# A residual conv block on one core: one pair recomputed in the last pass instead of two, a second pair of sums spilled and reloaded

## The chip, the cores and the metric

The kernel runs on one core of one Trainium2 chip. The metric is the device time of one execution in microseconds. The median of 3 runs of the kernel before is 548.7 us, the lowest 547.78 and the highest 549.61.

## The reference

The input x is float32 of shape (32, 64, 56, 56). The block computes x + relu(BN2(conv2(relu(BN1(conv1(g))))) + g), where g is x after a group norm of 32 groups (two channels in a group):

```python
identity = x
out = conv3x3(x, quantize_weight(w1, W_BITS), b1)
out = jax.nn.relu(batchnorm(out, gamma1, beta1))
out = conv3x3(out, quantize_weight(w2, W_BITS), b2)
out = batchnorm(out, gamma2, beta2)
out = jax.nn.relu(out + identity)
...
x = x + _L0_conv_ref(_gn(x), ...)
```

Both batch norms take their mean and variance over all 32 images, so that nothing of the output can be made before the second convolution of every image is done.

## The kernel before

**Pairs.** Two images of 64 channels fill the 128 partitions. There are NP = 16 such pairs; the data of one are 128 x 3136 float32, 1568 KB. Each conv splits its float32 input into a high and a low float16 part and runs 9 taps x 4 quadrants x 2 parts = 72 matmuls in each of 4 rounds (7 rows of each half image) that make a pair's sums in PSUM.

**Three passes.** Pass one loads x, takes the group norm statistics (DVE), splits (ACT makes the high part, DVE the low one), convolves, and keeps conv1's output in one of RES = 13 slots of SBUF; 3 pairs go out to DRAM (`y1_spill`). Pass two does the same with conv2 in the order `PAIR2`; its sums are put in the slots. Its last 3 steps need the pairs that were spilled, and they are loaded over the sums of steps 0, 1 and 2. Pass three, from the end of conv2 on, loads x again for each pair, computes relu(scale * sums + skip * x + bias) + x, and stores it. `ORDER3` gives the conv2 step that each turn u of pass three takes; "pair u" below is the pair of turn u. `x3[u]` is where its x is loaded.

**Where the 16 sets of sums are in pass three.** Pair 1's (`IN_PSUM`) stay in PSUM. Of the three sets that were overwritten, step 2's was stored to DRAM (`y2_spill`, L387) and is loaded back for pair 15 (`RELOADED`, L464). Steps 0 and 1 were lost: these are pairs 7 and 10 (`AGAIN`), and both convolutions are computed again for them from x. The other 12 sets are in slots.

**Three ways through pass three.**

- Ring pairs (1, 2, 3, 4, 11 to 15): ACT seeds a PSUM bank with scaled x (`seed`, L759), PE adds the sums through a diagonal matrix (`add_sums`, L1406), DVE finishes (`finish`, L1224). This is done in 4 rounds a pair, a bank each.
- Two-pass pairs (0, 5, 6, 8, 9), which need no PSUM: ACT scales the sums in place (`two_affine`, L747), DVE adds x (`sum_and_add`, L1202) and does the relu and the second addition (`relu_and_add`, L1208). Pair 0 is done in 5 pieces, the others in two halves. Pair 5's x lies partly in the spare ends of the slots (`IN_STRIPS`) and is loaded there early, during conv2.
- Recomputed pairs (7, 10): ACT makes act in float32 (`make_act1`, L775) and its high half (`make_hi1`, L781), DVE the low half (`again_low1`, L1230), PE convolves in 4 rounds (`again_round1`, L1429 and L1433), ACT and DVE split each round (`make_act2`, L792 and L794; `again_low2`, L1235), PE convolves again (`again_round2`, L1452) and adds x through `add_parts` (L1414), ACT seeds (`seed_again`, L799), DVE finishes (L1224).

**Transfers.** All loads and stores of pass three are issued by SP, in one order that is written out by hand (L443 to L478). SP waits ahead of each one for what it needs: a store for DVE's result, a load for the buffer to be free, either because DVE has read it (`wait_out`) or because a store out of it has landed (`wait_stored`). What stands behind a waiting transfer in this order waits with it. The orders of ACT (L802 to L846), DVE (L1239 to L1267) and PE (L1477 to L1496) are written out in the same way.

```python
            def wait_stored(u):
                sp.wait_ge(stored[u], 16 * STORES[u])

            def wait_out(u):
                if u in TWO_PASS:
                    sp.wait_ge(two_out, first_two(u) + 2)
                else:
                    sp.wait_ge(ring_out, nth(u, NQ - 1))
```

Of the kernel before, what the change touches and what calls it, by code (L numbers as in the profile page):

```python
# [23 lines left out]
def conv_block_kernel(nc, x, w1, b1, g1, be1, w2, b2, g2, be2, out):  # L24
# [61 lines left out]
    with ExitStack() as ctx:  # L86
# [262 lines left out]
        def _(sp):  # L349
# [70 lines left out]
            def store_first():  # L420
                for k in range(PARTS0):
# [5 lines left out]
            def store_two_pass(u):
                for k in range(2):
                    cols = half_of(u, k)
                    sp.wait_ge(two_out, first_two(u) + k + 1)  # L430
                    sp.dma_start(pair_view(out, PAIR3[u])[:, cols], out_of(u)[:, cols]).then_inc(stored[u], 16)
# [1089 lines left out]
```

## Time and profile before

| what | value |
|---|---|
| median of 3 runs | 548.7 us |
| the profiled execution's own time | 549.96 us |
| its span in the trace | 548.2 us |
| PE busy | 505.5 us (92%) |
| DVE busy | 442.6 us (81%) |
| ACT busy | 367.9 us (67%) |
| DMA of SP's queue (q1) | 91.19 MB, 44.7% of 16 engines' span |
| mean granted TensorE clock | 0.977 |

The span is cut into 40 equal slices on the page, of 13.7 us each. The end of conv2 lies in the 30th of them; the last ten hold pass three. Busy shares over the whole span mix passes with different limits, so pass three has to be read by itself, in stretches.

### The profile page before, as it was taken

Reading aid. Unit: us, or ns where it says so; the run is one execution under the profiler, and the core shown is the slowest. Engines: PE = TensorE matmul, PEld = TensorE weight load, DVE = VectorE, ACT = ScalarE, POOL = GpSimd, SP = SyncE. Lnnn points to the kernel's source line nnn. Section 1 sums busy time; section 2 is a strip of 40 time slices with the busy share of each in tenths; the row PEclk is TensorE's granted clock in tenths of the full one; section 3 lists DMA queues with packets and bytes.
Section 4 is the critical chain, followed back from the end, with each engine's and each line's share of the span. In section 5 each row is a group of like instructions: output and inputs, shape, how many; then the busy total and the mean of one; then the engine's idle time right before and its main releaser. Section 6 shows DMA issues by size and latency. Waiting matters only on the chain.

```text
span 548.2 us, 23785 instructions
## 1 busy us (share of the span) xinstructions
PE 505.5 (92%) x11037; PEld 429.0 (78%) x11037; DVE 442.6 (81%) x628; ACT 367.9 (67%) x402; POOL 96.4 (18%) x155
## 2 busy tenths in 40 slices
PE   3999999999999999999999999999968598999970
PEld 1899899999998896998988888888854277685540
DVE  8899989999999658988868988787869376896760
ACT  3799899989999845755665555566227577774650
POOL 2026366665662200210000000000010000000000
PEclk9899999999999999999999999999999899999995
DMA  8834775333441000002344000000659969299997
GB/s 289 322 126 128 271 274 178 133 125 131 162 160 58 8 7 7 4 2 121 130 158 181 26 4 2 4 4 4 205 221 354 381 245 325 98 359 426 416 423 314
DMA packets 24474, 92.99 MB, mean 170 GB/s; under 512 B 8248, under 2 KB 9656, under 8 KB 20664
## 3 DMA queue, kind: packets, MB, share of 16 engines
q1 hardware_dynamic: 24192, 91.19, 44.7%
q8 instruction: 86, 1.41, 1.1%
q10 hardware_dynamic: 184, 0.30, 0.2%
q14 instruction: 12, 0.10, 0.1%
HBM read 58.27 MB, written 32.28 MB: 165 GB/s over the span
## 4 chain that ended last, share of the span: by engine, by line
PE 84%; DMA 6%; DVE 4%; issue 2%; ACT 1%; SPq 0%; DVEq 0%; ACTq 0%
PE conv_ps L1310 69%; DMA slots<-in_x_dram 5%; PE conv_ps L1452 5%; PE conv_ps L1429 4%; PE conv_ps L1406 3%; DVE slots L1208 1%; PE conv_ps L1414 1%; DMA out_dram<-slots 1%; DVE slots L1202 1%; PE conv_ps L1273 1%; ACT split L591 0%; DVE small L920 0%; ACT conv_ps L759 0%; DVE slots L1224 0%; PE conv_ps L1308 0%
## 5 line engine op out<-in xcount | busy, mean ns | idle before, releaser
L1310 PE MATMUL conv_ps<-split,wmat 64*64 64x385 f16 (+3 forms) x9216 | 381.8, 325 | 1.6 <-ACT split L591 1.6
L1310 PEld LDWEIGHTS conv_ps<-split,wmat 64*64 64x64 bf16 x9216 | 342.8, 108 | 36.7 <-issue 2.3
L625 ACT ACTIVATE slots<-conv_ps,par,evac_scale 128x784 f32<-128x784 f32 x124 | 123.8, 999 | 96.2 <-PE conv_ps L1310 94.2
L1021 DVE BATCH_NORM_STATS2 bn_tup<-slots 128x6 f32<-128x392 f32 x166 | 81.9, 556 | 15.6 <-ACT slots L625 15.6
L920 DVE BATCH_NORM_STATS2 small<-slots 128x6 f32<-128x448 f32 x112 | 61.8, 615 | 0.7 <-DMA slots<-in_x_dram 0.7
L988 DVE TENSOR_TENSOR split<-slots,split 128x3136 f16<-128x3136 f32 (+4 forms) x36 | 57.2, 1608 | 4.6 <-ACT slots L599 1.0
L990 DVE SCALAR_TENSOR_TENSOR split<-slots,split 128x3248 f16<-128x3248 f32 (+3 forms) x18 | 53.6, 2979 | 2.3
L1406 PE MATMUL conv_ps<-slots,bn_tup 128*128 128x392 f32 x128 | 45.5, 516 | 9.9 <-ACT conv_ps L759 9.8
L1406 PEld LDWEIGHTS conv_ps<-slots,bn_tup 128*128 128x128 f32 x128 | 25.2, 199 | 30.0 <-issue 14.0
L974 DVE TENSOR_SCALAR slots<-slots,bn_w 128x3248 f32<-128x3248 f32 (+3 forms) x18 | 30.4, 1687 | 20.9 <-ACT split L583 20.5
L583 ACT ACTIVATE split<-slots,bn_w 128x3248 f16<-128x3248 f32 x14 | 43.1, 3082 | 0.0
L633 ACT ACTIVATE xa<-conv_ps,par,evac_scale 128x784 bf16<-128x784 f32 x40 | 39.7, 995 | 0.0
L1224 DVE SCALAR_TENSOR_TENSOR slots<-conv_ps,slots 128x784 f32<-128x784 f32 x20 | 19.4, 973 | 25.1 <-PE conv_ps L1406 14.4
L583 ACT ACTIVATE split<-slots,gn_b_all,gn_s_all 128x3136 f16<-128x3136 f32 x12 | 35.9, 2994 | 0.0
L546 POOL MEMSET bn_tup<- 128x192 f32 x1 | 0.3, 257 | 169.5 <-DVE bn_mv L1036 169.5
L974 DVE TENSOR_SCALAR slots<-slots,gn_s_all,gn_b_all 128x3136 f32<-128x3136 f32 (+4 forms) x19 | 26.4, 1396 | 1.5 <-ACT split L583 1.3
L526 POOL TENSOR_SCALAR small<-small 128x1 f32<-128x1 f32 x14 | 24.2, 1726 | 1.2
L591 ACT ACTIVATE split<-slots,gn_b_all,gn_s_all 128x784 f16<-128x784 f32 (+3 forms) x20 | 17.5, 901 | 0.6 <-DVE gn_b_all L951 0.6
L1308 PE MATMUL conv_ps<-split,wmat 64*64 64x55 f16 (+1 forms) x192 | 17.8, 187 | 0.0
L799 ACT ACTIVATE conv_ps<-conv_ps,again_w,bn_w 128x784 f32<-128x784 f32 x8 | 7.8, 975 | 14.6 <-PE conv_ps L1452 14.6
L515 POOL TENSOR_TENSOR small<-small 128x1 f32<-128x1 f32 x14 | 3.9, 278 | 77.4 <-DVE small L932 77.4
L524 POOL TENSOR_SCALAR small<-small 128x1 f32<-128x1 f32 x14 | 17.1, 1222 | 1.5
(161 smaller groups left out, 468.5 us busy)
## 6 DMA issues: line engine op xcount, KB each, us to landing
slots<-in_x_dram SPq DMA_DIRECT2D x51, 392.0 KB, 5.1
slots<-in_x_dram SPq DMA_DIRECT2D x10, 1568.0 KB, 9.3
out_dram<-slots SPq DMA_DIRECT2D x16, 784.0 KB, 14.5
split<-in_x_dram SPq DMA_DIRECT2D x4, 1568.0 KB, 15.3
out_dram<-slots SPq DMA_DIRECT2D x4, 1568.0 KB, 18.9
y_spill<-slots SPq DMA_DIRECT2D x3, 1624.0 KB, 7.0
slots<-y_spill SPq DMA_DIRECT2D x3, 1624.0 KB, 6.8
xa<-in_x_dram SPq DMA_DIRECT2D x3, 1568.0 KB, 9.7
```

What stands on the lines that cost most here:

```text
L526: nc.gpsimd.tensor_scalar(tmp(5), tmp(4), -0.5 * GN_GAIN, 1.5 * GN_GAIN, ALU.mult, ALU.add).then_inc(gn_pool, 1)
L583: nc.scalar.activation(whole(hi_of(t), ph), whole(slot_of(ph, t), ph), func, bias=bias, scale=scale).then_inc(hi_ready[ph], NQ)
L625: nc.scalar.activation(dst, src, ACT.Identity, bias=bias, scale=scale, accum_out=total).then_inc(evacuated[ph], 1)
L633: nc.scalar.activation(squares[n % 2], conv_ps[:, BUF[q], :, 0:CH], ACT.Square, bias=par[:, 0:1], scale=evac_scale[:, 0:1], accum_out=ysum ...
L920: ins = nc.vector.bn_stats(gn_tup[:, m, n, :], slots[:, t % RES, n * GN_CHUNK:(n + 1) * GN_CHUNK])
L974: ins = nc.vector.tensor_scalar(a, s, scale, bias, ALU.mult, ALU.add)
L988: ins = nc.vector.tensor_tensor(l, a, h, ALU.subtract)
L990: ins = nc.vector.scalar_tensor_tensor(out=l, in0=a, scalar=0.0, in1=h, op0=ALU.max, op1=ALU.subtract)
L1021: ins = nc.vector.bn_stats(bn_tup[:, 2 * (n - first) + s, :], rows[s])
L1310: return nc.tensor.matmul(bank[:, r0:r1, w0:w1], lhs, rows[:, top + r0:top + r1, w0 + kx - 1:w1 + kx - 1], start=n == 0 and part is hi_all ...
L1406: mm = nc.tensor.matmul(sums_in(k)[:, h], scale_diag, ys[:, h], start=False, stop=True, skip_group_check=True)
L1452: return nc.tensor.matmul(bank[:, r0:r1, w0:w1], lhs, rows[:, top + r0:top + r1, w0 + kx - 1:w1 + kx - 1], start=n == 0 and part == 0, sto ...
```

## The change

Pair 10 is no longer recomputed. A second set of conv2's sums is stored to DRAM during conv2, and two sets are loaded back in pass three, for the last two pairs (14 and 15). `AGAIN` holds pair 7 alone. Its x is loaded into `xa` during conv2, where pair 3's was; pair 3's x comes in five pieces behind the stores of pair 0, where pair 4's did. The two-pass pairs are 0, 4, 5 and 6: pair 4 was a ring pair, 8 and 9 become ring pairs. Pairs 4, 5 and 6 are done in halves between the rounds of pair 7. The order of the ring and of SP's transfers, and the buffers `x3`, are written anew to fit.

```diff
-    AGAIN = (7, 10)
-    RELOADED = NP - 1
-    ORDER3 = (SPILL, NP - 1, *range(SPILL + 1, SPILL + 6), 0, SPILL + 6, SPILL + 7, 1, *range(SPILL + 8, NP - 1), 2)
+    AGAIN = (7,)
+    RELOADED = {NP - 2: 4, NP - 1: 5}
+    ORDER3 = (SPILL, NP - 1, *range(SPILL + 1, SPILL + 6), 0, *range(SPILL + 6, NP - 1), 1, 2)
...
-    SLOT3 = [None if u == IN_PSUM or u in AGAIN else SLOT2[ORDER3[5 if u == RELOADED else u]] for u in range(NP)]
+    SLOT3 = [None if u == IN_PSUM or u in AGAIN else SLOT2[ORDER3[RELOADED.get(u, u)]] for u in range(NP)]
...
-    TWO_PASS = (0, 5, 6, 8, 9)
+    TWO_PASS = (0, 4, 5, 6)
...
-    STORES = [PARTS0, 2, 2, 2, 1, 2, 2, 2, 2, 2, 2, 1, 1, 1, 2, 4]
+    STORES = [PARTS0, 2, 2, 2, 2, 2, 2, 2, 1, 1, 1, 1, 1, 1, 2, 4]
...
-    IN_STRIPS = 5
+    IN_STRIPS = 4
...
-            slots[:, FREE], halves[0], halves[1], xa, slots[:, FREE], xa, slot3(2), slot3(0), xa, slot3(2), slots[:, FREE],
-            halves[0], halves[1], xa, slot3(2), slot3(0))]
-        again1 = [ap.bitcast(F16)[:, 0:2 * PIX].rearrange("p (h m) -> p h m", h=2) for ap in (halves[0], slot3(3))]
...
+            slots[:, FREE], halves[0], halves[1], slots[:, FREE], slot3(0), slots[:, FREE], slot3(2), xa, slot3(3), slot3(0),
+            slots[:, FREE], slot3(2), halves[0], halves[1], xa, slot3(3))]
...
-            for t in range(SPILL):
-                sp.wait_ge(evacuated[1], NQ * (t + 1))
-            sp.dma_start(y2_spill, slots[:, SLOT2[SPILL - 1], 0:PIX]).then_inc(y2_spilled, 16)
+            for n in range(SPILL - 1):
+                sp.wait_ge(evacuated[1], NQ * (n + 2))
+                sp.dma_start(y2_spill[n], slots[:, SLOT2[n + 1], 0:PIX]).then_inc(y2_spilled[n], 16)
             for t in range(SPILL):
                 sp.wait_ge(evacuated[1], NQ * (t + SPILL + 1))
                 sp.wait_ge(bn_seen[1], NQ * (t + 1))
-                if t == SPILL - 1:
-                    sp.wait_ge(y2_spilled, 16)
+                if t >= 1:
+                    sp.wait_ge(y2_spilled[t - 1], 16)
                 sp.dma_start(slots[:, SLOT2[NP - SPILL + t]], y1_spill[t]).then_inc(y1_loaded[t], 16)
...
-            load(3)
+            load(7)
...
-                    sp.dma_start(x3[4][:, cols], pair_view(x, PAIR3[4])[:, cols]).then_inc(x3_loaded[4], 16)
...
+                    sp.dma_start(x3[3][:, cols], pair_view(x, PAIR3[3])[:, cols]).then_inc(x3_loaded[3], 16)
+
+            def store_half(u, k):
+                cols = half_of(u, k)
+                sp.wait_ge(two_out, first_two(u) + k + 1)
+                sp.dma_start(pair_view(out, PAIR3[u])[:, cols], out_of(u)[:, cols]).then_inc(stored[u], 16)
...
+            def reload_sums(n):
+                u = NP - 2 + n
+                wait_stored(RELOADED[u])
+                sp.wait_ge(y2_spilled[n], 16)
+                sp.dma_start(slot3(u)[:, 0:PIX], y2_spill[n]).then_inc(y2_loaded[n], 16)
...
             store_first()
             store_ring(1)
             wait_stored(0)
-            load(7)
+            load(4)
             store_ring(2)
             store_ring(3)
             wait_out(3)
             load(5)
             wait_stored(2)
             load(6)
-            store_ring(4)
+            store_half(4, 0)
+            wait_stored(3)
+            load(8)
+            store_half(4, 1)
             wait_out(4)
+            load(9)
+            store_half(5, 0)
+            store_half(5, 1)
+            wait_out(5)
             load(10)
-            store_two_pass(5)
-            wait_out(5)
-            load(8)
-            store_two_pass(6)
+            reload_sums(0)
+            store_half(6, 0)
+            store_half(6, 1)
             wait_out(6)
-            load(9)
-            wait_stored(5)
-            sp.wait_ge(y2_spilled, 16)
-            sp.dma_start(slot3(RELOADED)[:, 0:PIX], y2_spill).then_inc(y2_loaded, 16)
+            load(11)
+            reload_sums(1)
             store_ring(7)
             wait_out(7)
-            load(11)
             load(12)
-            store_two_pass(8)
+            load(13)
+            store_ring(8)
             wait_out(8)
-            load(13)
-            store_two_pass(9)
-            wait_out(9)
+            load(15)
+            wait_stored(7)
             load(14)
-            wait_stored(7)
-            load(15)
-            for u in range(10, NP):
+            for u in range(9, NP):
                 store_ring(u)
...
             make_act1(0)
-            seed(4, 0)
-            seed(4, 1)
             make_hi1(0)
-            seed(4, 2)
-            seed(4, 3)
+            two_affine(4, 0)
+            two_affine(4, 1)
+            make_act2(0, 0)
             two_affine(5, 0)
+            make_act2(0, 1)
             two_affine(5, 1)
-            make_act2(0, 0)
+            make_act2(0, 2)
             two_affine(6, 0)
-            make_act2(0, 1)
+            make_act2(0, 3)
             two_affine(6, 1)
-            make_act2(0, 2)
-            make_act2(0, 3)
-            seed_again(0, 0)
-            make_act1(1)
-            seed_again(0, 1)
-            make_hi1(1)
-            seed_again(0, 2)
-            two_affine(8, 0)
-            seed_again(0, 3)
-            two_affine(8, 1)
-            make_act2(1, 0)
-            two_affine(9, 0)
-            make_act2(1, 1)
-            two_affine(9, 1)
-            make_act2(1, 2)
-            make_act2(1, 3)
             for q in range(NQ):
-                seed_again(1, q)
-            for u in range(11, NP):
+                seed_again(0, q)
...
-            dve.wait_ge(x3_loaded[4], 16 * PARTS0)
-            finish(4, 0)
-            finish(4, 1)
             again_low1(0)
-            finish(4, 2)
-            finish(4, 3)
-            for r in range(2):
-                u = (5, 8)[r]
-                for q in range(NQ):
-                    two_pass(u, q)
-                    again_low2(r, q)
-                for q in range(NQ):
-                    two_pass(u + 1, q)
-                    finish(AGAIN[r], q)
-                    if (r, q) == (0, 1):
-                        again_low1(1)
-            for u in range(11, NP):
+            two_pass(4, 0)
+            two_pass(4, 1)
+            again_low2(0, 0)
+            two_pass(4, 2)
+            again_low2(0, 1)
+            two_pass(4, 3)
+            two_pass(5, 0)
+            again_low2(0, 2)
+            two_pass(5, 1)
+            again_low2(0, 3)
+            two_pass(5, 2)
+            two_pass(5, 3)
+            finish(7, 0)
+            two_pass(6, 0)
+            finish(7, 1)
+            two_pass(6, 1)
+            two_pass(6, 2)
+            finish(7, 2)
+            two_pass(6, 3)
+            finish(7, 3)
+            for u in range(8, NP):
...
-                pe.wait_ge(ring_out, nth((4, AGAIN[0])[r], q))
+                pe.wait_ge(ring_out, nth(3, q))
...
-            for u in (2, 3, 4):
+            for u in (2, 3):
...
-            again_round1(1, 0)
             add_parts(0, 3)
-            for q in range(1, NQ):
-                again_round1(1, q)
-            again_round2(1, 0)
-            for q in range(1, NQ):
-                again_round2(1, q)
-                add_parts(1, q - 1)
-            add_parts(1, 3)
-            for u in range(11, NP):
+            for u in range(8, NP):
```

Along with these, `y2_spill`, `y2_spilled` and `y2_loaded` are made twofold, and the waits for pair 7's inputs name the new neighbours.

How the instructions stand on the engines, in pass three. First SP's transfers. Before, from the stores of pair 1 to those of pair 9 (L441 and L431 are stores, L397 loads of x, L464 the reload):

```order
L441 DMA out_dram<-slots 128x1568 x4
L397 DMA xa<-in_x_dram 128x1680
L397 DMA slots<-in_x_dram 128x3136
L441 DMA out_dram<-slots 128x3136
L397 DMA slots<-in_x_dram 128x3136
L431 DMA out_dram<-slots 128x1456
L431 DMA out_dram<-slots 128x1680
L397 DMA xa<-in_x_dram 128x3136
L431 DMA out_dram<-slots 128x1568 x2
L397 DMA slots<-in_x_dram 128x3136
L464 DMA slots<-y_spill 128x3136
```

And in the changed kernel, from the stores of pairs 2 and 3 to the second reload (L446 and L430 are the stores, L436 the reloads):

```order
L446 DMA out_dram<-slots 128x1568 x4
L397 DMA slots<-in_x_dram 128x3136 x2
L430 DMA out_dram<-slots 128x1456
L397 DMA slots<-in_x_dram 128x3136
L430 DMA out_dram<-slots 128x1680
L397 DMA slots<-in_x_dram 128x3136
L430 DMA out_dram<-slots 128x1568 x2
L397 DMA slots<-in_x_dram 128x3136
L436 DMA slots<-y_spill 128x3136
L430 DMA out_dram<-slots 128x1568 x2
L397 DMA slots<-in_x_dram 128x3136
L436 DMA slots<-y_spill 128x3136
```

Behind the two loads that follow pair 3's stores, SP now waits for half a two-pass pair (128x1456), not for a whole ring pair; and ahead of pair 6's two stores (the last x2 of halves in each fence) it issues five loads of x and a reload, where it issued four loads, one of them of 128x1680.

Second, DVE's order from the end of pair 3 or 4 on. Before (L1224 finishes a round, L1230 and L1235 belong to the recomputed pair, L1202 and L1208 to two-pass pairs):

```order
L1224 SCALAR_TENSOR_TENSOR slots<-conv_ps,slots 128x784 x2
L1230 TENSOR_TENSOR split<-split 128x3136
L1224 SCALAR_TENSOR_TENSOR slots<-conv_ps,slots 128x784 x2
L1202 SCALAR_TENSOR_TENSOR slots<-slots,skip_s 128x1456
L1235 SCALAR_TENSOR_TENSOR split<-conv_ps,split 128x2x448
L1208 SCALAR_TENSOR_TENSOR slots<-slots 128x1456
L1235 SCALAR_TENSOR_TENSOR split<-conv_ps,split 128x2x392
L1202 SCALAR_TENSOR_TENSOR slots<-xa,skip_s,slots 128x1680
L1235 SCALAR_TENSOR_TENSOR split<-conv_ps,split 128x2x392
L1208 SCALAR_TENSOR_TENSOR slots<-slots,xa 128x1680
```

In the changed kernel the same place reads (L1208 finishes a round, L1214 and L1219 belong to the recomputed pair, L1186 and L1192 to two-pass pairs):

```order
L1208 SCALAR_TENSOR_TENSOR slots<-conv_ps,slots 128x784 x4
L1214 TENSOR_TENSOR split<-split 128x3136
L1186 SCALAR_TENSOR_TENSOR slots<-slots,skip_s 128x1456
L1192 SCALAR_TENSOR_TENSOR slots<-slots 128x1456
L1219 SCALAR_TENSOR_TENSOR split<-conv_ps,split 128x2x448
L1186 SCALAR_TENSOR_TENSOR slots<-slots,skip_s 128x1680
L1219 SCALAR_TENSOR_TENSOR split<-conv_ps,split 128x2x392
L1192 SCALAR_TENSOR_TENSOR slots<-slots 128x1680
L1186 SCALAR_TENSOR_TENSOR slots<-slots,skip_s 128x1568
L1219 SCALAR_TENSOR_TENSOR split<-conv_ps,split 128x2x392
```

No ring round stands between the low half and the rounds of the recomputed pair any more, and the first two-pass half is finished ahead of the first split of a round instead of around it.

## Rows read from the trace of the kernel before

**Rows 1.** The page's second part: the span in 40 slices, DMA's busy tenths and GB/s.

```profile
DMA  8834775333441000002344000000659969299997
GB/s 289 322 126 128 271 274 178 133 125 131 162 160 58 8 7 7 4 2 121 130 158 181 26 4 2 4 4 4 205 221 354 381 245 325 98 359 426 416 423 314
```

**Rows 2.** Busy time in stretches of pass three; the header names the columns.

```profile
core 0: us, PE busy (x) PEld busy (x) DVE busy (x) ACT busy (x) POOL busy (x), PEclk, DMA share, GB/s
409.50:415.00 5.50, 5.19 (x11) 2.86 (x12) 5.40 (x8) 5.50 (x7) 0.27 (x1) 0.69 0.71 221
415.00:440.00 25.00, 16.65 (x45) 9.00 (x44) 13.71 (x15) 15.88 (x14) 0.00 (x0) 0.88 1.02 390
440.00:450.00 10.00, 10.00 (x215) 7.60 (x217) 7.88 (x6) 6.93 (x7) 0.00 (x0) 0.95 0.47 196
450.00:465.00 15.00, 13.44 (x312) 12.17 (x303) 10.96 (x8) 12.05 (x11) 0.00 (x0) 1.00 0.95 321
465.00:480.00 15.00, 14.13 (x350) 10.00 (x352) 12.33 (x9) 11.37 (x9) 0.00 (x0) 1.00 0.30 121
480.00:505.00 25.00, 24.23 (x505) 17.76 (x498) 19.39 (x15) 14.15 (x15) 0.00 (x0) 1.00 1.01 390
505.00:546.50 41.50, 26.48 (x80) 14.74 (x78) 21.20 (x22) 17.99 (x19) 0.00 (x0) 0.88 0.97 402
```

**Rows 3.** What SP's queue waited for, 440 to 480 us: total, times, longest.

```profile
SPq L431 <- DVE slots L1208: 29.0, 4, 10.7
```

**Rows 4.** SP's issues in order of time: start, length, line, transfer, count.

```profile
249.41 0.33 SPq L387 DMA_DIRECT2D y_spill<-slots  x1
...
452.81 7.20 SPq L431 DMA_DIRECT2D out_dram<-slots  x2
460.06 0.46 SPq L397 DMA_DIRECT2D xa<-in_x_dram  x1
467.96 11.39 SPq L431 DMA_DIRECT2D out_dram<-slots  x2
479.39 0.46 SPq L397 DMA_DIRECT2D slots<-in_x_dram  x1
```

**Rows 5.** ACT in order of time around 425 to 440 us.

```profile
425.30 1.01 ACT L759 ACTIVATE conv_ps<-xa,skip_b,skip_s 128x784 f32<-128x784 f32 x1 [0.31 <-DVE slots L1224]
432.09 3.00 ACT L775 ACTIVATE split<-slots,again_w,gn_s_all 128x3136 f32<-128x3136 f32 x1 [5.78 <-DMA slots<-in_x_dram]
...
436.87 2.98 ACT L781 ACTIVATE split<-slots,again_w,gn_s_all 128x3136 f16<-128x3136 f32 x1
```

**Rows 6.** The chain that ended last, 475 us to the end: start, length, what.

```profile
478.69 9.09 PE conv_ps L1429 x214
487.78 6.12 PE conv_ps L1452 x141
...
506.41 14.58 DMA slots<-in_x_dram
522.17 10.79 PE conv_ps L1406 x32
```

**Rows 7.** DVE's operations of the stretch, one of each kind, in order of time.

```profile
442.36 3.42 DVE L1230 TENSOR_TENSOR split<-split 128x3136 f16<-128x3136 f32 x1
...
453.48 0.97 DVE L1235 SCALAR_TENSOR_TENSOR split<-conv_ps,split 128x784 f16<-128x784 f32 x1 [0.69 <-ACT conv_ps L794]
...
460.44 1.84 DVE L1202 SCALAR_TENSOR_TENSOR slots<-slots,skip_s 128x1568 f32<-128x1568 f32 x1
465.26 0.97 DVE L1224 SCALAR_TENSOR_TENSOR slots<-conv_ps,slots 128x784 f32<-128x784 f32 x1 [2.98 <-PE conv_ps L1414]
466.15 1.78 DVE L1208 SCALAR_TENSOR_TENSOR slots<-slots 128x1568 f32<-128x1568 f32 x1
```

**Rows 8.** Busy time in three stretches of 5 us, for PEclk.

```profile
430.00:435.00 5.00, 0.00 (x0) 0.00 (x0) 0.53 (x1) 2.91 (x1) 0.00 (x0) 0.92 1.01 422
435.00:440.00 5.00, 3.87 (x6) 2.18 (x7) 0.81 (x1) 5.00 (x5) 0.00 (x0) 0.50 1.04 436
440.00:445.00 5.00, 5.00 (x53) 2.83 (x55) 3.69 (x3) 4.88 (x4) 0.00 (x0) 0.90 0.54 229
```

**Rows 9.** DMA issues, the last store of all (533 to 535 us): size, time to landing.

```profile
out_dram<-slots SPq DMA_DIRECT2D x1, 392.0 KB, 13.7
```

More of the change, by code:

```diff
@@ L219, in conv_block_kernel @@
         y1_loaded = [sem(f"y1_loaded{n}") for n in range(SPILL)]
-        y2_spilled = sem("y2_spilled")
+        y2_spilled = [sem(f"y2_spilled{n}") for n in range(SPILL - 1)]
         strips_loaded = sem("strips_loaded")
-        y2_loaded = sem("y2_loaded")
+        y2_loaded = [sem(f"y2_loaded{n}") for n in range(SPILL - 1)]
         skip_coef = sem("skip_coef")
@@ L290, in conv_block_kernel @@
         x3 = [ap[:, 0:PIX] for ap in (
-            slots[:, FREE], halves[0], halves[1], xa, slots[:, FREE], xa, slot3(2), slot3(0), xa, slot3(2), slots[:, FREE],
-            halves[0], halves[1], xa, slot3(2), slot3(0))]
-        again1 = [ap.bitcast(F16)[:, 0:2 * PIX].rearrange("p (h m) -> p h m", h=2) for ap in (halves[0], slot3(3))]
-        again_fp32 = [ap[:, 0:PIX] for ap in (halves[1], slot3(4))]
-        again2 = [ap.bitcast(F16).rearrange("p (h m) -> p h m", h=2) for ap in (halves[1], slot3(4))]
+            slots[:, FREE], halves[0], halves[1], slots[:, FREE], slot3(0), slots[:, FREE], slot3(2), xa, slot3(3), slot3(0),
+            slots[:, FREE], slot3(2), halves[0], halves[1], xa, slot3(3))]
+        again1 = [ap.bitcast(F16)[:, 0:2 * PIX].rearrange("p (h m) -> p h m", h=2) for ap in (halves[0],)]
+        again_fp32 = [ap[:, 0:PIX] for ap in (halves[1],)]
+        again2 = [ap.bitcast(F16).rearrange("p (h m) -> p h m", h=2) for ap in (halves[1],)]
         spread_ps = stat_ps[:, 0:C]
@@ L424, in store_first @@
                     sp.dma_start(pair_view(out, PAIR3[0])[:, cols], out_of(0)[:, cols]).then_inc(stored[0], 16)
-                    sp.dma_start(x3[4][:, cols], pair_view(x, PAIR3[4])[:, cols]).then_inc(x3_loaded[4], 16)
[L427 to L431, printed above, removed]
+                    sp.dma_start(x3[3][:, cols], pair_view(x, PAIR3[3])[:, cols]).then_inc(x3_loaded[3], 16)
[8 more added lines that the diff above has]
+                sp.dma_start(slot3(u)[:, 0:PIX], y2_spill[n]).then_inc(y2_loaded[n], 16)
             def store_ring(u):
@@ L755, in seed @@
                 if k == 0:
-                    sc.wait_ge(x3_loaded[u], 16 * (PARTS0 if u == 4 else 1))
+                    sc.wait_ge(x3_loaded[u], 16 * (PARTS0 if u == 3 else 1))
                 sc.wait_ge(ring_out, nth(u, k) - NQ)
@@ L770, in make_act1 @@
                 sc.wait_ge(x3_loaded[AGAIN[r]], 16)
-                if r == 0:
-                    sc.wait_ge(ring_out, nth(2, NQ - 1))
-                else:
-                    sc.wait_ge(stored[4], 16 * STORES[4])
+                sc.wait_ge(ring_out, nth(2, NQ - 1))
                 nc.scalar.activation(again_fp32[r], x3[AGAIN[r]], ACT.Identity, bias=bias, scale=scale).then_inc(again_act1, 1)
@@ L1244, in _ @@
             for u in (1, 2, 3):
[L1245 removed]
+                dve.wait_ge(x3_loaded[u], 16 * (PARTS0 if u == 3 else 1))
                 for k in range(NQ):
                     finish(u, k)
[L1248 to L1250 removed]
             again_low1(0)
[L1252 to L1264 removed]
+            two_pass(4, 0)
[19 more added lines that the diff above has]
+            for u in range(8, NP):
                 dve.wait_ge(x3_loaded[u], 16)
@@ L1399, in add_sums @@
                 pe.wait_ge(scale_diag_ready, 2)
-                if u == RELOADED:
-                    pe.wait_ge(y2_loaded, 16)
+                if u in RELOADED:
+                    pe.wait_ge(y2_loaded[u - (NP - 2)], 16)
                 for k in range(NQ):
@@ L1485, in _ @@
                 add_parts(0, q - 1)
-            again_round1(1, 0)
             add_parts(0, 3)
-            for q in range(1, NQ):
-                again_round1(1, q)
-            again_round2(1, 0)
-            for q in range(1, NQ):
-                again_round2(1, q)
-                add_parts(1, q - 1)
-            add_parts(1, 3)
-            for u in range(11, NP):
+            for u in range(8, NP):
                 add_sums(u)
```

8 lines of the change are left out of this document (2 added, 6 removed).

## The prediction

> **What bounds the kernel now.** I read the page's slices first. In passes one and two DMA's digits are low and TensorE's work covers them; in pass three they are mostly 9, but for a hole near its middle [rows 1]. So pass three is read by itself, in stretches [rows 2]. From 480 us on the 16 DMA engines are as good as full (shares 1.01 and 0.97) while PE, DVE and ACT all have time to spare. The last store is issued 13.7 us before it lands [rows 9], so the end is set by the queue of transfers, not by the engine that made the last result. The chain says the same: its last long pieces are a load that lands 14.58 us after its issue and the ring behind it [rows 6].
>
> So pass three lasts as long as its transfers, plus the time in which the queue was empty. The unit is one pair, 1568 KB. Before, from 409.5 us on, it moves 16 stores, 11.54 loads (12 pairs are loaded then; of pair 5, 1456 of 3136 columns are there already) and one reload: 28.54 units. Empty time by the shares of [rows 2]: 0.29 x 5.5 = 1.6 at the start, 0.53 x 10 = 5.3, 0.05 x 15 = 0.75, 0.70 x 15 = 10.5 and 0.03 x 41.5 = 1.2 at the end, 19.3 in all. The other 117.7 us of the 137 make **4.12 us a unit**.
>
> Why it is empty: SP waits 29.0 us in 4 waits for the second half of DVE's two-pass work [rows 3]. The two stores of pair 6 are issued at 467.96 and some 11 us later, and the loads that would fill the queue stand behind them, the next at 479.39 [rows 4]. DVE is late because the recomputed pair 7, between whose rounds it works, began late: ACT sat 5.78 us until pair 7's x had landed at 432 [rows 5], and finished its high half at 439.85.
>
> **The change part by part.**
>
> Transfers: one reload is added, nothing else changes in size (the first load into `xa` is pair 7's and not pair 3's; pair 3's pieces take pair 4's place behind pair 0's stores; the strips now hold pair 4's columns). 29.54 units: **+4.1 us**. Bounds: 3.99 at 402 GB/s, the stretch from 505 us, and 5.0 at 321 GB/s, the lowest of the stretches without a hole [rows 2]; I take the mean of the pass, which holds both. The Trainium skill ("DMA: Bandwidth & Descriptors", Specifications) gives about 358 GB/s as a core's limit at HBM, which speaks against a change that adds traffic; by it the unit is 4.49 us, an estimate. This case's trace disagrees: 390 to 402 GB/s over long stretches, 436 in one of 5 us [rows 2, 8].
>
> The second spill, during conv2: at nothing. It goes next to the one at 249.41 [rows 4], where DMA's digits are 2 and 0 [rows 1]. Without that cover the load of the second spilled pair would wait for it, one unit, 4 us at most, with whole pairs of conv2 ahead of it.
>
> The recompute removed: PE loses 9.09 us (three rounds) + 6.12 us (two) and its other three rounds, some 24 us, and 3 for its x; ACT about 18 (two whole operations of 3, twelve of 1), DVE 11.2 (3.42 + 8 x 0.97 [rows 7]). None of it is credited by itself, since the queue sets the end; it counts only by what it does to the empty time. The two ring pairs that take its place on PE cost 10.79/8 = 1.35 us a round [rows 6], 5.4 a pair, against 8.2 us for their load and store: the ring stays covered.
>
> **The empty time after.** I walk the new order with these durations. Up to the end of pair 3's seeds (425.30 + 1.01 = 426.3 [rows 5]) nothing moves. Pair 7's x has been there since conv2, so its float32 form (3.0) ends at 429.3, its high half (2.98) at 432.3 [rows 5] where it was 439.85, its low half (3.42) at 435.8. From 432.3 DVE is the limit: 3.42 for the low half, six halves at 1.84 + 1.78 = 21.7, four splits and four finishes at 0.97 [rows 7] = 7.8: 32.9 us, to about 465; PE's 8 rounds at 3.04 [rows 6] take 24 and the parts 3. By DVE's order the halves of pairs 4, 5 and 6 are out at about 439, 446, 451, 455, 461 and 465.
>
> Against that, the queue: with pair 6's load, issued at 432, 7.54 units have gone since 409.5, done at 409.5 + 1.6 + 7.54 x 4.12 = 442.2. At 439 half of pair 4 and load 8 (1.46 units) extend it to 448.2; at 446, 1.54 units to 454.6; at 451, 0.5 to 456.6; at 455, the half, load 10 and a reload (2.5) to 466.9; at 461 to 469; at 465 pair 6's half, load 11, the second reload, pair 7's stores and loads 12 and 13 (5.5) to 491.7. The margins are 3, 2, 4, 1.4, 6 and 4 us. Then SP waits for pair 7's stores to land before load 14, some 15 us, with pairs 9 to 11's stores behind it, but with 25 us of transfers issued ahead. The last result should be ready about 14 us before the queue is done.
>
> So the middle's 16.55 us of empty time go. With margins this thin I keep **2 us**: one for the clock, since PE is idle from about 430 and the first round starts at 432.3 and then waits for the low half (before, after idle from 430 to 435, the granted clock was 0.50, the 1.2 GHz level, for 5 us [rows 8]), one for what 450 to 465 shows with a queue in use, 0.05 x 15. Bounds: 0, and 8, half of what is there now.
>
> **Sum.** -16.55 + 2 + 4.1 = -10.4 us. The profiled execution took 549.96 us (span 548.2); 539.5 then, and the median shown is 1.3 lower: **538.2 us**. The other way round: 409.5 + 29.54 x 4.12 + 1.6 + 1.2 + 2 + the 1.7 after 546.5 = 537.7 of span, the same.
>
> **Rivals.**
>
> *The hole only shrinks* (14%). DVE and PE run late against the thin margins, each late half holds SP with two loads behind it, and 7 to 8 us stay empty: 543.5 to 545. For: the present order lost its time in just this way. Against: pair 7 starts 7.5 us earlier and SP has more issued ahead.
>
> *The clock stays low* (4%, slower). If TensorE is granted 1.2 GHz through the recompute, because every round waits on DVE, its 8 rounds take 6.1 us each, 24 more; pair 7's result, with the ring and four loads behind it, comes at about 489 and the queue runs dry. My walk then holds some 20 us of empty time in the middle: 548.7 - 16.55 + 20 + 4.1 = 556. It ends slower than before once more than 12.4 us are empty there, that is, when the rounds take some 5.3 us each. Against: at 440 to 445 the grant was back at 0.90 and then 1.00, with the same mix of waits [rows 8, 2]. The Trainium skill ("TensorE: Matmul & The Clock Gate", What's actually happening) has the throttled state as the default that activity releases; by that, the trace agrees.
>
> *The rate is worse with two more streams under way* (3%). At 4.49 us a unit 29.54 units take 132.6 us; with 4.8 of empty time and 1.7 at the end the span is 548.6: no change. That is what the skill's 358 GB/s named above would give; the rows so far bear out 390.
>
> *The queue's margins hold better than thought* is part of the forecast: no empty time, and 3.99 us a unit, give 538.2 - 2 - 3.8 = 532.4.
>
> **How the numbers follow.** The forecast, 532 to 543, has 75%, the first rival 14, the second 4, the third 3; 4 are for what I have not thought of, on either side. The predicted time is the likeliest, 538 us. The range takes in the first rival: 532 to 545.5. A measurement of this kernel can tell some 0.3% (1.6 us) from no change. Faster by more: 75 + 14 + 2 = 91%; within it: 4 (the third rival and a little); slower: 5.
>
> **What would show it.** Right: the DMA share between 440 and 480 above 0.9, no wait of SP for a two-pass half over 6 us that leaves the share under 0.8; pair 7's high half done by 433; its first finish at about 455; GB/s near 390 from 432 on; the last store issued more than 10 us before it lands; PE busy less by some 16 us (27 less two ring pairs at 5.4). Wrong: a hole near 446 or 455, where the margins are thinnest; a clock under 0.9 past 440; a wait of the ring for load 12 or 14 that outlasts the queue; more than 4.3 us a unit. A time over 545 would say the queue was not what set the end.

## The result and the profile after

| | kernel before | changed kernel |
|---|---|---|
| median, us | 549.15 (547.78 to 551.05, 4 runs) | 533.03 (532.38 to 534.51, 4 runs) |
| profiled execution, its own time | 549.96 | 532.38 |
| its span | 548.2 | 530.6 |
| PE, DVE, ACT busy | 505.5, 442.6, 367.9 | 488.6, 432.8, 355.4 |
| bytes of SP's queue | 91.19 MB | 94.40 MB |

The ratio is 0.9708 (0.9671 to 0.9745): faster, by 16 us of the medians and 17.6 us of the span. Run again later, the same kernel gave a median of 533.92 us (0.9722, 0.9689 to 0.9756) and, in the profiled execution, a span of 533.0, so two medians of one kernel differ by 0.9 us and two spans by 2.4.

The page's slices of the changed kernel; in [rows 1] the 33rd digit is 6 and the 35th is 2:

```profile
DMA  8834775533333000004343300000065999999998
GB/s 291 340 130 128 253 256 173 202 126 139 130 134 128 12 7 7 2 33 166 136 167 133 125 4 2 4 4 2 4 236 206 346 387 419 400 401 417 431 428 337
```

From the 32nd slice on DMA stays at 9, up to the last, an 8. The same in stretches, against [rows 2]:

```profile
core 0: us, PE busy (x) PEld busy (x) DVE busy (x) ACT busy (x) POOL busy (x), PEclk, DMA share, GB/s
409.50:415.00 5.50, 5.35 (x11) 3.04 (x12) 5.40 (x7) 5.48 (x7) 0.11 (x1) 0.67 0.73 222
415.00:440.00 25.00, 19.08 (x248) 12.67 (x250) 19.66 (x18) 19.07 (x15) 0.00 (x0) 1.00 1.02 388
440.00:450.00 10.00, 8.98 (x221) 8.56 (x215) 9.60 (x7) 10.00 (x10) 0.00 (x0) 1.00 1.01 417
450.00:465.00 15.00, 13.75 (x262) 9.36 (x253) 13.07 (x11) 6.68 (x7) 0.00 (x0) 1.00 1.02 402
465.00:480.00 15.00, 15.00 (x47) 8.68 (x46) 12.31 (x13) 12.13 (x13) 0.00 (x0) 1.00 1.00 399
480.00:505.00 25.00, 19.42 (x52) 10.50 (x51) 13.05 (x14) 11.25 (x13) 0.00 (x0) 0.86 1.02 428
505.00:528.90 23.90, 10.63 (x32) 5.83 (x32) 7.80 (x8) 6.54 (x7) 0.00 (x0) 0.79 0.96 405
```

Between 440 and 480 the share was 0.47, 0.95 and 0.30 and is 1.01, 1.02 and 1.00. Empty time is now 0.27 x 5.5 at the start and 0.04 x 23.9 at the end: 2.5 us, where it was 19.3.

What fills it are the half pairs. The two halves of pair 4 are stored one by one, each with a load behind it; those of pairs 5 and 6 go out two in a row, with a load and a reload behind each pair (SP's issues in order of time):

```profile
438.88 0.34 SPq L430 DMA_DIRECT2D out_dram<-slots  x1
439.27 0.43 SPq L397 DMA_DIRECT2D slots<-in_x_dram  x1
446.02 0.34 SPq L430 DMA_DIRECT2D out_dram<-slots  x1
446.41 0.43 SPq L397 DMA_DIRECT2D slots<-in_x_dram  x1
450.37 4.81 SPq L430 DMA_DIRECT2D out_dram<-slots  x2
455.23 0.48 SPq L397 DMA_DIRECT2D slots<-in_x_dram  x1
455.80 0.98 SPq L436 DMA_DIRECT2D slots<-y_spill  x1
462.05 4.68 SPq L430 DMA_DIRECT2D out_dram<-slots  x2
466.78 0.47 SPq L397 DMA_DIRECT2D slots<-in_x_dram  x1
```

SP still waits for DVE's two-pass halves, but no longer than 6.3 us at a time (in [rows 3] up to 10.7, with the queue running empty behind it), and its longest wait for a buffer is the 10.0 us for pair 7's stores. These are SP's waits from 405 us to the end: total, times, longest.

```profile
SPq L430 <- DVE slots L1192: 28.7, 6, 6.3
...
SPq L397 <- DMA out_dram<-xa: 10.0, 1, 10.0
```

The earlier start is seen on ACT, where [rows 5] has 5.78 us of idle time and x at 432 (ACT in order of time):

```profile
425.15 1.01 ACT L765 ACTIVATE conv_ps<-slots,skip_b,skip_s 128x784 f32<-128x784 f32 x1 [0.31 <-DVE slots L1208]
426.10 2.99 ACT L778 ACTIVATE split<-xa,again_w,gn_s_all 128x3136 f32<-128x3136 f32 x1
428.99 2.98 ACT L783 ACTIVATE split<-xa,again_w,gn_s_all 128x3136 f16<-128x3136 f32 x1
```

The chain that ended last now goes through the queue from 469 us on (start, length, what):

```profile
469.13 15.91 DMA out_dram<-xa
...
485.06 18.63 DMA xa<-in_x_dram
...
503.71 1.02 ACT conv_ps L765
...
504.86 10.79 PE conv_ps L1395 x32
```

The last result is ready at 516.6 us, and the last store lands 13.4 us after its issue:

```profile
out_dram<-slots SPq DMA_DIRECT2D x1, 392.0 KB, 13.4
```

### The profile page after: what moved, and what is told of

It reads as the page before. It is cut to its first block, busy times and chain, and to the rows that moved or that the text cites. A ratio compares the mean times of both kernels' runs of the same rounds, so it can differ in the third digit from the quotient of the medians.

```text
span 530.6 us, 22461 instructions
## 1 busy us (share of the span) xinstructions
PE 488.6 (92%) x10393; PEld 402.3 (76%) x10393; DVE 432.8 (82%) x622; ACT 355.4 (67%) x394; POOL 95.6 (18%) x155
## 3 DMA queue, kind: packets, MB, share of 16 engines
q1 hardware_dynamic: 23936, 94.40, 47.0%
## 4 chain that ended last, share of the span: by engine, by line
PE 80%; DMA 7%; DVE 6%; ACT 2%; issue 1%; SPq 0%; DVEq 0%; ACTq 0%
PE conv_ps L1299 71%; DMA xa<-in_x_dram 4%; PE conv_ps L1395 3%; DMA out_dram<-xa 3%; PE conv_ps L1418 2%; PE conv_ps L1441 2%; DVE slots L1192 1%; DVE slots L1186 1%; DMA slots<-in_x_dram 1%; DVE slots L1208 1%; DVE split L1214 1%; ACT split L778 1%; ACT split L783 1%; DVE xa L1208 1%; PE conv_ps L1262 1%
## 5 line engine op out<-in xcount | busy, mean ns | idle before, releaser
L1299 PE MATMUL conv_ps<-split,wmat 64*64 64x385 f16 (+3 forms) x9216 | 381.4, 325 | 1.1 <-ACT split L597 1.1
L1299 PEld LDWEIGHTS conv_ps<-split,wmat 64*64 64x64 bf16 x9216 | 330.8, 107 | 48.2 <-issue 2.1
L1395 PE MATMUL conv_ps<-slots,bn_tup 128*128 128x392 f32 x160 | 56.2, 512 | 7.4 <-ACT conv_ps L765 7.3
L1395 PEld LDWEIGHTS conv_ps<-slots,bn_tup 128*128 128x128 f32 x160 | 31.3, 198 | 32.0 <-issue 11.7
L1208 DVE SCALAR_TENSOR_TENSOR slots<-conv_ps,slots 128x784 f32<-128x784 f32 x24 | 23.2, 974 | 7.1 <-PE conv_ps L1395 7.1
L765 ACT ACTIVATE conv_ps<-slots,skip_b,skip_s 128x784 f32<-128x784 f32 x24 | 23.7, 1005 | 5.3 <-DVE slots L1208 3.6
L532 POOL TENSOR_SCALAR small<-small 128x1 f32<-128x1 f32 x14 | 24.1, 1720 | 1.2
L1208 DVE SCALAR_TENSOR_TENSOR slots<-conv_ps,split 128x784 f32<-128x784 f32 x12 | 11.7, 974 | 10.7 <-PE conv_ps L1395 10.7
L765 ACT ACTIVATE conv_ps<-split,skip_b,skip_s 128x784 f32<-128x784 f32 x12 | 11.6, 999 | 11.9 <-DMA split<-in_x_dram 6.0
L1418 PE MATMUL conv_ps<-split,wmat 64*64 64x385 f16 (+3 forms) x288 | 13.2, 326 | 5.2 <-ACT split L783 2.7
```

Of the source, the lines that this page charges most:

```text
L765: nc.scalar.activation(sums_in(k), banked(x3[u], u, k), ACT.Identity, bias=skip_b[:, i:i + 1], scale=skip_s[:, i:i + 1]).then_inc(seeded, 1)
L1208: nc.vector.scalar_tensor_tensor(out=banked(out_of(u), u, k), in0=sums_in(k), scalar=0.0, in1=banked(x3[u], u, k), op0=ALU.max, op1=ALU.ad ...
L1299: return nc.tensor.matmul(bank[:, r0:r1, w0:w1], lhs, rows[:, top + r0:top + r1, w0 + kx - 1:w1 + kx - 1], start=n == 0 and part is hi_all ...
L1395: mm = nc.tensor.matmul(sums_in(k)[:, h], scale_diag, ys[:, h], start=False, stop=True, skip_group_check=True)
```

## The experiments

The theory: pass three lasts as long as its transfers plus the time in which the queue is empty, and the change gains by emptying less. Three parts of it could bring that: DVE's order of pieces, pair 7's early x, and one recompute fewer. The rivals are that the relief of the engines pays (one recompute less), and that the end hangs on the last result and not on the queue.

### What one pair of traffic costs

```diff
-                store_ring(u)
+                if u != 10:
+                    store_ring(u)
```

> The changed kernel without the stores of pair 10 (the turn u = 10; those rows of the output stay unwritten): one unit of 1568 KB less in pass three, no engine's work changed. If the queue of transfers sets the end, the time falls by what one unit takes in a full queue: 29.54 units in the 116.9 us that were not empty make 3.96 us, so 533.0 - 4.0 = 529.0 us. Rival: the chain of results sets the end (the last store is issued 13 us before it lands, but the store's own time might be what it waits for); then nothing moves, 533.0.

Measured: 529.85 us (528.85 to 531.84), ratio to before 0.9647 (0.9624 to 0.967), span 527.0. That is 3.2 us less in the median and 3.6 less in the span than the changed kernel, for one unit of 29.54 and no other work. Against the second median of the changed kernel it is 4.1. Transfers set the end, and a unit in a full queue costs 3.2 to 4.1 us, by these numbers no more than the mean of 4.12 us that the prediction took.

### Pair 7 late again

ACT waits, ahead of pair 7's act, for the stores of pair 2, about the time at which pair 7's x came before.

```diff
                 sc.wait_ge(x3_loaded[AGAIN[r]], 16)
+                sc.wait_ge(stored[2], 16 * STORES[2])
```

> The changed kernel, but ACT begins pair 7 only when pair 2's stores have landed, near 433 us in place of 426.1: about the 432.09 at which it began before. All else as in the change. By the queue theory the half pairs come some 6 us later against margins of 1.4 to 4 us at that place, so the queue runs empty for 4 to 7 us in the middle: 537 to 540 us. Rival: pair 7's early input is worth nothing, since 13 us of slack at the end absorb a late start: 533.0. Third reading: if all 7 us come through, 540.

Measured: 539.28 us (538.51 to 541.49), ratio 0.9821 (0.9798 to 0.9844). ACT's piece and three of the stretches (columns as in [rows 2]):

```profile
433.17 3.00 ACT L779 ACTIVATE split<-xa,again_w,gn_s_all 128x3136 f32<-128x3136 f32 x1 [7.16 <-DMA out_dram<-slots]
```

```profile
440.00:450.00 10.00, 10.00 (x260) 9.01 (x255) 8.46 (x5) 6.94 (x7) 0.00 (x0) 0.81 0.53 200
450.00:465.00 15.00, 14.94 (x332) 12.16 (x328) 14.56 (x12) 11.78 (x11) 0.00 (x0) 1.00 0.94 332
465.00:480.00 15.00, 14.41 (x122) 8.76 (x115) 13.83 (x14) 10.34 (x12) 0.00 (x0) 1.00 1.01 390
```

A start 7.1 us later costs 6.2 us: 4.7 us of empty queue at 440 to 450 (0.47 x 10), 0.9 behind it, and a stretch in which the share is 0.94 and only 332 GB/s move, where the changed kernel has 402. The early start of pair 7 is needed. Part of its price can be the clock: PE was idle from 430 to 435, the grant was 0.50 (the 1.2 GHz level) from 435 to 440 and 0.62 in the next 5 us, where the changed kernel had 1.00. How much of the 6.2 us that makes was not tried.

### DVE alternating as before

```diff
-            two_pass(4, 0)
-            two_pass(4, 1)
-            again_low2(0, 0)
...
+            for q in range(NQ):
+                two_pass(4, q)
+                again_low2(0, q)
+            for q in range(NQ):
+                two_pass(5, q)
+                finish(7, q)
+            for q in range(NQ):
+                two_pass(6, q)
```

> The changed kernel with DVE's order of the kernel before put back: one step of a two-pass pair and one step of pair 7 by turns (pair 4 with the splits, pair 5 with the finishes, pair 6 after them). Same instructions, same transfers, one recompute. By the queue theory the second halves come out later, SP waits with loads behind it, and a walk gives some 9 us of empty time: 540 to 543 us. Rival: the gain came from the recompute that was taken out, not from the order: within 1.5 us of 533.0.

Measured: 545.15 us (544.9 to 546.44), ratio 0.992 (0.9903 to 0.9936): 12.1 us of the gain are gone, more than expected. The stretches, SP's longest wait, and DVE where it stands still:

```profile
440.00:450.00 10.00, 10.00 (x242) 8.17 (x234) 8.20 (x7) 10.00 (x10) 0.00 (x0) 1.00 0.85 322
450.00:465.00 15.00, 11.73 (x215) 7.35 (x215) 7.75 (x6) 4.12 (x4) 0.00 (x0) 0.89 0.60 225
465.00:480.00 15.00, 8.43 (x45) 4.37 (x36) 13.74 (x12) 6.69 (x8) 0.00 (x0) 0.93 0.70 253
```

```profile
SPq L430 <- DVE slots L1192: 38.8, 6, 11.2
```

```profile
458.56 0.97 DVE L1208 SCALAR_TENSOR_TENSOR xa<-conv_ps,xa 128x784 f32<-128x784 f32 x1 [6.03 <-PE conv_ps L1391]
```

Empty time is 1.5 + 6.0 + 4.5 = 12.0 us, which is the loss. DVE stood idle 6.03 us ahead of pair 7's first finish, while the second step of a half of pair 5, which needed nothing from PE, was queued behind it. So the order of pieces is worth 12 us here, the largest effect that one edit had.

### DVE's order alone, on the kernel before

Both recomputes are kept; only DVE's list is written in the new manner.

```diff
             for r in range(2):
                 u = (5, 8)[r]
-                for q in range(NQ):
-                    two_pass(u, q)
-                    again_low2(r, q)
-                for q in range(NQ):
-                    two_pass(u + 1, q)
+                two_pass(u, 0)
+                two_pass(u, 1)
+                again_low2(r, 0)
+                two_pass(u, 2)
+                again_low2(r, 1)
+                two_pass(u, 3)
+                two_pass(u + 1, 0)
...
```

> The kernel before, both recomputes, all transfers and ACT's, PE's and SP's orders kept; only DVE's order is changed to that of the changed kernel: the two-pass halves of pairs 5 and 6 (and of 8 and 9) as early as possible between the splits of pair 7 (and 10), the finishes after them. By the queue theory most of the 16.55 us of empty time in the middle goes (a walk leaves 3 to 6), with one unit less than the changed kernel moves: 549.15 - 11 = 538 us, between 534 and 541. Rival: the second recompute is what made the kernel slow (PE, ACT and DVE cannot do two in pass three in time): within 3 us of 549.

Measured: 540.72 us (539.61 to 543.71), ratio 0.9849 (0.9818 to 0.988); its span is 8.7 us under that of the kernel before, half of the change's 17.6.

```profile
440.00:450.00 10.00, 10.00 (x262) 8.60 (x264) 9.96 (x8) 7.11 (x6) 0.00 (x0) 1.00 0.53 199
450.00:465.00 15.00, 12.94 (x292) 10.94 (x286) 14.03 (x10) 11.22 (x11) 0.00 (x0) 1.00 0.98 373
465.00:480.00 15.00, 11.56 (x287) 8.22 (x280) 5.19 (x3) 8.40 (x6) 0.00 (x0) 0.99 0.84 333
480.00:505.00 25.00, 24.88 (x519) 17.87 (x521) 20.50 (x15) 13.36 (x13) 0.00 (x0) 0.94 0.89 340
```

The hole at 465 to 480 shrinks from 10.5 to 2.4 us. The one at 440 to 450 stays (ACT begins pair 7 at 430.07, still 4 us behind the changed kernel), and a new one opens behind 475, where pair 7's last round waits on PE behind pair 10's first (2.85 us of that wait is a pause of PE, see the last section):

```profile
480.83 0.97 DVE L1224 SCALAR_TENSOR_TENSOR slots<-conv_ps,slots 128x784 f32<-128x784 f32 x1 [6.96 <-PE conv_ps L1424]
```

### The early x alone, on the kernel before

Pair 7's x goes into `xa` during conv2, pair 3's comes in pieces; pair 10's load moves behind pair 5's stores, as its buffer demands.

```diff
-            load(3)
+            load(7)
...
-                    sp.dma_start(x3[4][:, cols], pair_view(x, PAIR3[4])[:, cols]).then_inc(x3_loaded[4], 16)
+                    sp.dma_start(x3[3][:, cols], pair_view(x, PAIR3[3])[:, cols]).then_inc(x3_loaded[3], 16)
...
-            load(10)
+            load(8)
             store_two_pass(5)
             wait_out(5)
-            load(8)
+            load(10)
```

> The kernel before with one part of the change: pair 7's x is loaded into xa during conv2 in place of pair 3's, pair 3's comes in pieces behind pair 0's stores, pair 4's whole behind pair 1's; to make room pair 10's load moves behind pair 5's stores. Both recomputes and DVE's order stay. The queue theory: pair 7 starts 6 us earlier, but SP still waits for the second halves and pair 10 now starts some 10 us later against its own rounds, so the empty time does not shrink (a walk gives 18 us for 15): 547 to 553 us. Rival: the early input is a gain by itself: 543 to 545.

Measured: 549.93 us (549.06 to 553.07), ratio 1.0021 (0.9998 to 1.0045): nothing.

```profile
440.00:450.00 10.00, 9.20 (x273) 7.91 (x275) 5.93 (x5) 6.93 (x7) 0.00 (x0) 1.00 1.02 411
450.00:465.00 15.00, 14.03 (x314) 10.89 (x306) 11.05 (x8) 6.19 (x6) 0.00 (x0) 1.00 0.67 249
465.00:480.00 15.00, 10.02 (x196) 7.17 (x200) 8.11 (x5) 11.85 (x7) 0.00 (x0) 0.77 0.14 55
```

```profile
SPq L431 <- DVE slots L1208: 43.6, 6, 15.9
```

The hole at 440 is gone and stands at 450 to 480, where SP waits up to 15.9 us for a half (5.0 + 12.9 us empty). But the edit did two things. Pair 7's x came early, and pair 10's came late, and ACT stood still for it, with three of pair 7's seeds behind it in its list:

```profile
465.98 3.00 ACT L775 ACTIVATE slots<-slots,again_w,gn_s_all 128x3136 f32<-128x3136 f32 x1 [6.94 <-DMA slots<-in_x_dram]
```

In the kernel before ACT began this piece at 462.48 without waiting for x. So the run shows that this exchange of buffers gains nothing; what the early x alone is worth with the old order of DVE stays open, since no run has it without the late pair 10.

### Both together with two recomputes

The edits of the last two, and on PE pair 7's last `add_parts` ahead of pair 10's first round:

```diff
-            again_round1(1, 0)
             add_parts(0, 3)
-            for q in range(1, NQ):
+            for q in range(NQ):
                 again_round1(1, q)
```

> A version that might beat both: the kernel before with two recomputes (28.54 units, one less than the changed kernel), DVE's order of the fourth run of this study, pair 7's x early, and on PE the last addition of pair 7's x ahead of pair 10's first round (in the fourth run it stood behind it and the finish of pair 7 came 7 us late). If the holes of the fourth run (4 us at 440, 5.5 us at 475 to 485) go, 540.7 - 9 = 532, and at best a unit below the changed kernel, 529. If two recomputes cannot keep the queue fed, 535 to 541.

Measured: 539.95 us (538.1 to 541.93), ratio 0.9843 (0.9802 to 0.9885). It is the worse of the two outcomes that were named.

```profile
465.00:480.00 15.00, 13.11 (x291) 9.97 (x295) 9.90 (x6) 10.45 (x8) 0.00 (x0) 0.89 0.85 320
480.00:505.00 25.00, 22.02 (x484) 16.41 (x473) 16.34 (x12) 12.42 (x13) 0.00 (x0) 1.00 0.85 321
```

With a unit less to move it takes 6 to 7 us more than the changed kernel, and only 0.8 less than the run with DVE's order alone: for 40 us the share is 0.85 and the rate 320 GB/s, while SP waits for pair 7's stores and then for the halves of pairs 8 and 9. ACT waited for pair 10's x here too, ahead of pair 7's seeds:

```profile
461.90 3.00 ACT L775 ACTIVATE slots<-slots,again_w,gn_s_all 128x3136 f32<-128x3136 f32 x1 [5.18 <-DMA slots<-in_x_dram]
```

In this form two recomputes don't keep the queue fed. How much of that is the second recompute's own work and how much the late x of pair 10 was not separated.

### No recompute at all

Three sets of sums are spilled and reloaded, pair 7 is a ring pair: 30.54 units.

```diff
-    AGAIN = (7,)
-    RELOADED = {NP - 2: 4, NP - 1: 5}
+    AGAIN = ()
+    RELOADED = {NP - 3: 4, NP - 2: 5, NP - 1: 6}
```

> No pair is recomputed: all three overwritten sets are spilled in conv2 and loaded back in pass three, pair 7 is a plain ring pair. One unit more than the changed kernel (30.54), some 27 us of PE, 18 of ACT and 11 of DVE less. By the queue theory the engines' relief is worth nothing and the unit costs 3.96: 537 us (535.5 to 538.5). Rival: each recompute taken out gives time back as the first one did: below 530.

Measured: 535.37 us (535.27 to 535.52), ratio 0.9759 (0.9728 to 0.9791), 2.3 us above the changed kernel, 1.5 above its second median, and 0.1 under the range that was expected. The intervals of the ratios overlap (0.9671 to 0.9745 and 0.9689 to 0.9756 for the changed kernel), so the loss is small and near what can be told.

```profile
440.00:450.00 10.00, 0.00 (x0) 0.00 (x0) 9.90 (x6) 1.44 (x1) 0.00 (x0) 0.50 1.01 402
450.00:465.00 15.00, 9.50 (x23) 5.25 (x24) 11.96 (x10) 7.11 (x8) 0.00 (x0) 0.72 1.01 418
465.00:480.00 15.00, 8.86 (x27) 4.56 (x25) 7.31 (x8) 4.29 (x5) 0.00 (x0) 0.96 1.01 429
480.00:505.00 25.00, 18.21 (x48) 9.90 (x48) 11.70 (x12) 11.63 (x12) 0.00 (x0) 0.84 1.01 428
```

PE is idle for all of 440 to 450 and the share is 1.01 all the same: once the queue is full, relief of the engines gains nothing. Taking out the last recompute saves no time and rather costs some. That the first one gained because of the hole alone fits this, but no run takes out the first recompute and leaves all else as before.

### Slack of the last result

Fifteen DVE operations that nobody needs, 7.1 us, ahead of pair 14's finishes.

```diff
+                if u == 14:
+                    for n in range(15):
+                        nc.vector.bn_stats(small[:, 6 * n:6 * n + 6], x3[11][:, 0:CH])
```

> The changed kernel with 15 statistics operations of 0.55 us (8.3 us) on DVE ahead of pair 14's finishes; their output goes to spare columns. The last result, ready 13 us before the queue is done, then comes 5 us before it. By the queue theory 533 to 535 us. Rival: the chain of pair 14's load, ring and store sets the end: 541.

Measured: 534.18 us (532.9 to 534.99), ratio 0.9735 (0.9701 to 0.977); 0.3 us from the second median of the changed kernel, 1.2 from the first.

```profile
504.19 7.11 DVE L1256 BATCH_NORM_STATS2 small<-slots 128x6 f32<-128x392 f32 x15
```

DVE had been waiting for PE there, so of the 7.1 us only 3.3 reached the last result: it came at 519.9 us instead of 516.6, and the span is 531.1 instead of 530.6. Up to that delay the end doesn't hang on the last result, although the chain of waits runs through it; a longer one was not tried.

### Pair 7's x in pieces, after conv2

The changed kernel with the two loads exchanged: pair 3's x whole during conv2, pair 7's in five pieces behind pair 0's stores.

```diff
-            load(7)
+            load(3)
...
-                    sp.dma_start(x3[3][:, cols], pair_view(x, PAIR3[3])[:, cols]).then_inc(x3_loaded[3], 16)
+                    sp.dma_start(x3[7][:, cols], pair_view(x, PAIR3[7])[:, cols]).then_inc(x3_loaded[7], 16)
```

> The changed kernel with pairs 3 and 7 exchanging their ways in: pair 3's x is loaded into xa during conv2, as before the change, and pair 7's comes in five pieces behind pair 0's stores (the last issued at 416.9 and landing near 422, 4 us ahead of the 426.1 at which ACT wants it). By the queue theory only the start of pair 7 counts, so nothing moves: within 1.5 us of the changed kernel in this batch. Rival: having the input in during conv2 is what brings the gain: slower by some 3 to 6 us.

Measured: 534.16 us (532.2 to 537.7), ratio 0.9741 (0.9703 to 0.978). In the same comparison the changed kernel itself ran once more:

> The changed kernel as it is, beside the next one: 533.0 us, within 1.5.

Measured: 533.92 us (531.76 to 535.68). The two are the same. What counts is not that the x comes during the second convolution, but that it is there when ACT is through with pair 3's seeds: in this run's trace ACT began pair 7 at 429.19, right behind them and without a wait (426.10 in the changed kernel; 3 us of difference were there when pass three began).

None of these kernels beat the changed one, apart from the one that leaves a pair's output out. Taken out of the changed kernel one at a time, DVE's order is worth 12.1 us and the early start of pair 7 6.2, together 18.3 and so more than the whole change (16.1): they remove the same empty time. The third part, one recompute fewer with nothing else changed, was not run.

## Why the prediction was right, and where it was off

**What bounds the kernel.** Right. One unit less of traffic shortens it by 3.2 to 4.1 us, one more, with the last recompute gone, lengthens it by 1.5 to 2.3 (near the noise), and a last result that comes 3.3 us later doesn't move it beyond the noise.

**The empty time goes.** Right, -16.8 us for the -16.55 of the sum. The walk over DVE's order hit its times: halves at 439, 446, 451, 455, 461 and 465 were forecast, and DVE ended them at 438.9, 446.0, 450.3, 454.8, 462.0 and 466.4. The high half of pair 7 was forecast for 432.3 and ended at 431.97, its first finish for 455 and began at 454.73. SP's wait for pair 7's stores was 10.0 us and not 15, with the queue full behind it. The last result was to be ready 14 us before the end of the queue; it came at 516.6, about 13.

**The 2 us kept.** Too many. The clock didn't fall in the recompute: at 430 to 435 the grant was 1.00 (below) and stayed there up to 480, and the thin margins held in both traces of this kernel. The run with pair 7 late shows how thin they are, since 7.1 us of delay open a hole of 4.7 us at once; the prediction gave the first of them 3 us.

**The traffic.** This is the term that was mis-sized, 4.12 us a unit. The sum had +4.1 for the added unit. The queue's full time was 119.4 us (409.5 to 528.9) less 2.5 of empty time, 116.9 us for 29.54 units, 3.96 each; against the 117.7 us of before it is -0.8 and not +4.1. The second trace of the same kernel gives 4.01 a unit (3.2 us empty, 118.6 full), +0.9. The mean of before held slow stretches that were counted as busy. In 450 to 465 [rows 2] the share was 0.95 at 321 GB/s, where the changed kernel has 402 and in its second trace 376: 1.4 to 2.3 us by themselves. In 480 to 505 the share was 1.01 at 390, where the changed kernel has 428: over 2 us more, with the queue full in both, and why is not shown. So the one unit costs 3.2 to 4.1 us, and the busy time that was there before shrank by another 3 to 4, which the share of empty time doesn't tell. The prediction named this value, 3.99 us a unit and no empty time, as its best case (532.4) and put the likeliest time 5.8 us above it. The measured time lies 1 us inside the lower end of its range. With the sizes as measured: -16.8 - 0.8 = -17.6 us, the span's difference, as it must be, since both terms are read from the two spans.

**The engines.** PE's busy time fell by 16.9 us, where 16 were forecast. It was credited with nothing by itself, and the run without any recompute agrees.

**The rivals.** The shrinking hole didn't come; its mechanism, a late half that holds SP with loads behind it, is what the runs with pair 7 late and with DVE alternating show, at 539.3 and 545.2 us. The low clock didn't come: the recompute's rounds ran at 1.00. Nor did the low rate. The limit of about 358 GB/s that the Trainium skill gives for a core ("DMA: Bandwidth & Descriptors", Specifications) did not bind this kernel, which runs on one core alone: the trace disagrees, with 388 to 428 GB/s in each stretch from 415 us to 505, and the run without a recompute kept 402 to 429 from 440 to 505 with one unit more.

## What to carry to other kernels

Where a queue of transfers sets the end, look for the stretches in which it runs dry, and follow the wait back to the engine whose order of pieces is late: writing that order anew gave half the gain by itself and cost nothing. A store or load that is added to get rid of work that starves the queue costs only its own bytes at the full rate, but the next one of its kind, with no hole left, brings nothing. Parts that remove the same hole don't add: try each alone and all but each, and look in the trace at what else the edit moved, since a load that comes early for one pair can make another's late.

## What the runs showed of the hardware

**A DMA share near 1 is not one rate.** In the stretch from 450 to 465 the share was 0.95 at 321 GB/s in the kernel before [rows 2], 0.94 at 332 in the run with pair 7 late and 0.98 at 373 in the one with DVE's order alone, against 1.02 at 402 in the changed kernel. A queue with few transfers issued ahead may be one cause, but not the only one: the second trace of the changed kernel has 1.00 at 376 there, with the queue as full. The cause was not tried. Read GB/s beside the share.

**The rate of a full queue varies.** The changed kernel moves 417 GB/s from 440 to 450 and 402 from 450 to 465, while the recompute's rounds run, 399 from 465 to 480, when they are over, and 428 behind that. The run without any recompute moves 402 from 440 to 450 with PE idle, and 429 from 465 on. So the rounds on PE don't explain it, and what does stays open.

**PE pauses inside the recomputed rounds, and the profile shows nothing that it waits for.** The chain of waits of the run with DVE's order alone has such a piece:

```profile
476.26 2.85 issue
```

In the changed kernel there are two, of 1.02 us at 444.79 and 0.67 at 457.35. The cause stays open.

**The clock.** Busy time of 430 to 435 in the changed kernel:

```profile
430.00:435.00 5.00, 1.98 (x72) 1.60 (x72) 3.31 (x2) 5.00 (x3) 0.00 (x0) 1.00 1.02 423
```

PE had work for 1.98 us there and the grant stayed at 1.00, the 2.4 GHz level, and also in the next 5 us; in [rows 8] it had none, and 0.50 followed. In the run without a recompute PE was idle from 440 to 450 with the grant at 0.50, and came back to 0.96 at 465 to 480. Work in part of a stretch is no guarantee: in the run with pair 7's x in pieces PE was busy for 2.46 us from 430 to 435 at a grant of 0.96, and the next 5 us had 0.70:

```profile
435.00:440.00 5.00, 4.70 (x128) 3.80 (x131) 4.83 (x2) 3.24 (x3) 0.00 (x0) 0.70 1.04 434
```
